# Seeding a second mask per column tile in the attention stage: ScalarE for the even key tiles, VectorE for some odd ones

## What is computed

```python
def proj(W):
    return (x @ W.T).reshape(B, S, H, D).transpose(0, 2, 1, 3)
q, k, v = (proj(Wq), proj(Wk), proj(Wv))
scores = jnp.einsum('bhsd,bhtd->bhst', q, k) * scale
scores = jnp.where(mask[None, None, :, :], -jnp.inf, scores)
attn = jax.nn.softmax(scores, axis=-1)
out = jnp.einsum('bhst,bhtd->bhsd', attn, v)
```

## Time and profile before

| | |
|---|---|
| median of three runs | 1149.29 us (1147.65 to 1151.28) |
| the profiled execution | 1151.16 us |
| its span | 1149.4 us |
| mean granted TensorE clock | 0.993 of full speed |
| PE busy | 1112.2 us |
| ACT busy | 789.9 us |
| DVE busy | 759.8 us |
| POOL busy | 509.5 us |
| mask matmuls L1191 on PE | 386 weight loads; 332 matmul records, mean 383 ns |
| mask copies L1378 on ACT | 124, mean 602 ns |
| row reductions L1646 on DVE | 512, mean 684 ns |
| exponentials L1372 on ACT | 512, mean 598 ns |

### The profile page before, as it was taken

The page is one execution under the profiler, slowest core; times in us unless marked ns, Lnnn a source line. Parts: engine busy times, 40 slices in busy tenths (PEclk is TensorE's granted clock), DMA queues, the critical chain, the costliest instruction groups (busy, mean ns, idle before and its releaser), DMA issues.

```text
span 1149.4 us, 23356 instructions
## 1 busy us (share of the span) xinstructions
PE 1112.2 (97%) x7466; PEld 780.0 (68%) x7520; DVE 759.8 (66%) x2265; ACT 789.9 (69%) x1752; POOL 509.5 (44%) x837
## 2 busy tenths in 40 slices
PE   8899999999999999999899999989999999999988
PEld 4333434445344453444339999979999999999968
DVE  5887786787867878678744443455555555677547
ACT  2478787887878878788596567646666666666645
POOL 7413254756747567575643663552222222232220
PEclk9999999999999999999899999999999999999999
DMA  8663938558475583754747699664566666633536
GB/s 216 191 198 124 278 122 243 163 175 257 136 229 179 170 241 131 233 179 141 262 135 232 196 278 335 194 149 117 156 181 201 194 194 204 206 54 64 166 92 220
DMA packets 101617, 213.66 MB, mean 186 GB/s; under 512 B 10917, under 2 KB 71341, under 8 KB 93046
## 3 DMA queue, kind: packets, MB, share of 16 engines
q1 hardware_dynamic: 86038, 192.42, 52.6%
q0 software_dynamic: 14304, 18.69, 8.8%
q10 hardware_dynamic: 1152, 1.05, 0.4%
HBM read 239.28 MB, written 74.29 MB: 273 GB/s over the span
## 4 chain that ended last, share of the span: by engine, by line
PE 62%; DMA 5%; issue 4%; POOL 4%; DVE 3%; ACT 2%; another core or an unknown queue 0%; POOLq 0%; DVEq 0%; ACTq 0%
PE bank L1104 31%; PE bank L1206 6%; PE bank L1173 6%; PE bank L1187 5%; DMA x<-yout,rows 4%; PE bank L1191 3%; PE bank L1150 2%; PE bank L1159 1%; PE bank L1224 1%; PE bank L1119 1%; PE bank L1264 1%; POOL x L1993 1%; ACT pt L1372 1%; PE bank L1244 1%; DVE junk L1646 1%
## 5 line engine op out<-in xcount | busy, mean ns | idle before, releaser
L1646 DVE CUSTOM_DVE_ANT_0 junk<-bank,mneg 128x512 bf16<-128x512 f32 x512 | 332.3, 684 | 110.6 <-PE bank L1173 107.9
L1372 ACT ACTIVATE pt<-bank 128x512 f32<-128x512 f32 x512 | 294.2, 598 | 64.1 <-PE bank L1187 25.9
L1993 POOL DMA_INDIRECT x<-yout,rows x78 | 123.8, 1587 | 298.6 <-ACT yout L1456 252.1
L1104 PE MATMUL bank<-hid,w 128*128 128x256 f32 x1872 | 243.7, 287 | 4.7 <-DVE hid L1794 4.7
L1104 PEld LDWEIGHTS bank<-hid,w 128*128 128x128 f32 x1872 | 230.4, 191 | 6.7 <-issue 4.8
L1794 DVE TENSOR_TENSOR hid<-full,hid 128x256 fp32r<-128x256 f32 x312 | 134.2, 436 | 140.3 <-ACT full L1451 134.7
L1446 ACT ACTIVATE hid<-bank,biases 128x256 fp32r<-128x256 f32 x312 | 150.5, 482 | 96.1 <-PE bank L1104 88.7
L1451 ACT ACTIVATE full<-bank,biases 128x256 f32<-128x256 f32 x312 | 149.8, 480 | 0.5 <-DVE hid L1794 0.5
L1191 PE MATMUL bank<-mneg,identb 128*128 128x512 bf16 x332 | 127.2, 383 | 0.0
L1206 PE MATMUL bank<-pt,vaug 128*17 128x512 f32 x1024 | 123.3, 599 | 1.8
L1104 PE MATMUL bank<-w,hid 128*128 128x256 f32 x936 | 122.3, 284 | 2.7 <-DVE hid L1794 2.7
(11 more groups left out here) (184 smaller groups left out, 1459.9 us busy)
## 6 DMA issues: line engine op xcount, KB each, us to landing
w<-split_weights SPq DMA_DIRECT2D x80, 1024.0 KB
w<-split_weights SPq DMA_DIRECT2D x40, 2048.0 KB
split_weights<-w_parts SPq DMA_DIRECT2D x64, 512.0 KB
w_parts<-in_W SPq DMA_DIRECT2D x64, 256.0 KB
split_parts<-parts SPq DMA_DIRECT2D x28, 384.0 KB, 2.6
rows<-routed SPq DMA_DIRECT2D x39, 258.0 KB, 4.1
stacks<-split_parts SPq DMA_DIRECT2D x36, 256.0 KB, 6.8
qst<-split_parts SPq DMA_DIRECT2D x24, 256.0 KB, 6.3
```

The lines of the kernel that those rows point to most:

```text
L1104: product = T.matmul(ps, w[p], x[q], start=(k == 0 and n == 0), stop=(k == len(weights) - 1 and n == 2))
L1372: A.activation(pt[n % len(pt)][:, :], ps[:, :], ACT.Exp, scale=float(D) ** -0.5).then_inc(exped.sem, 1)
L1646: V.tensor_tensor_reduce(junk[n % 2][:, :], ring_bank(step)[0][:, :], mneg[:, 0, st, :], 1.0, FLOOR, ALU.add, ALU.max, rowmax[gi % 2][:, h ...
L1993: G.indirect_dma_start(x2_dram, bass.IndirectOffsetOnAxis(ap=rows[j % NS][:, tt, E + 1:E + 2].bitcast(U32), axis=0), yout[j % NY][:, tt], ...
```

## The change

More column products are seeded, and fewer L1191 are issued.

- In key tiles 0 and 2 of groups 1 to 31, ACT seeds two products in place of one: head 3 as before, and head 1. The added copy stands behind the exponential of head 3 of the tile before.
- In key tiles 1 and 3 ACT seeds head 0 as before. In those groups whose number modulo 4 is 0 or 1, below group 30, DVE seeds one more, head 2: a `tensor_copy` of the mask (128 x 512, bf16 to f32 in PSUM) behind the reduction of the row product two before the one that precedes it (`ROWS_AHEAD` = 3). It waits for the masks and for the bank's earlier user, and counts up a semaphore of its own, `seeded_too`, on which the product then waits.
- For DVE a product counts as seedable only if the bank's earlier user lies at least three row (or column) products back (`early`).

Counted through the order of the steps, ACT has 186 copies in place of 124 (62 more, two for each of 31 groups), DVE has 30 new ones (two for each of the groups 1, 4, 5, 8, 9, ... 28, 29), and L1191 is issued 386 - 92 = 294 times.

```diff
+ROWS_AHEAD = 3
...
-    seed_after = {}
+    rows_before, n = {}, 0
+    for step in order:
+        n += step[0] == "row"
+        if step[0] == "col":
+            rows_before[step[1:]] = n
+
+    def early(user, at):
+        if user[0] == "row":
+            return row_place[user[1:]] <= rows_before[at] - ROWS_AHEAD
+        return user[0] == "col" and col_place[user[1:]] <= col_place[at] - ROWS_AHEAD
+
+    seed_after, seed_behind = {}, {}
     for gi in range(1, GROUPS):
         for kt in range(ST):
-            for hh in ((3, 2, 1, 0), (0, 1, 2, 3))[kt % 2]:
-                place = col_place[gi, kt, hh]
+            by_vector = kt % 2 and gi % NG < 2 and gi < GROUPS - 2
+            many = kt % 2 == 0
+            free = []
+            for hh in ((3, 1, 2, 0), (0, 2, 1, 3))[kt % 2]:
                 user = ring_before(("col", gi, kt, hh))
-                if user[0] == "row" or user[0] == "col" and col_place[user[1:]] <= place - SEED_AHEAD:
-                    seed_after[cols_at[place - SEED_AHEAD]] = gi, kt, hh
-                    break
+                if user[0] == "row" or user[0] == "col" and col_place[user[1:]] <= col_place[gi, kt, hh] - SEED_AHEAD:
+                    free.append((gi, kt, hh))
+            for at in free[:2 if many else 1]:
+                seed_after[cols_at[col_place[at] - SEED_AHEAD]] = at
+            for at in [at for at in free[1:] if by_vector and early(ring_before(("col", *at)), at)][:1]:
+                seed_behind[rows_at[rows_before[at] - ROWS_AHEAD]] = at
...
-                seed = (gi, kt, hh) in seeded.value
-                if seed:
+                seed = (gi, kt, hh) in seeded.value or (gi, kt, hh) in seeded_too.value
+                if (gi, kt, hh) in seeded.value:
                     pe.wait_ge(*seeded.at((gi, kt, hh)))
+                elif seed:
+                    pe.wait_ge(*seeded_too.at((gi, kt, hh)))
                 else:
                     pe.wait_ge(*freed)
...
                                        rowmax[gi % 2][:, hh, st:st + 1]).then_inc(max_found.sem, 1)
+                after = seed_behind.get((gi, hh, st))
+                if after:
+                    ps, freed = ring_bank(("col", *after))
+                    dve.wait_ge(masks_made, MASKS)
+                    dve.wait_ge(*freed)
+                    V.tensor_copy(ps[:, :], mneg[:, 1, after[1], :]).then_inc(seeded_too.sem, 1)
```

More of the change, by code:

```diff
@@ L765, in ring_before @@
         return ring_users[n] if n >= 0 else None
-    seed_after = {}
+    rows_before, n = {}, 0
[8 more added lines that the diff above has]
+    seed_after, seed_behind = {}, {}
     for gi in range(1, GROUPS):
         for kt in range(ST):
-            for hh in ((3, 2, 1, 0), (0, 1, 2, 3))[kt % 2]:
-                place = col_place[gi, kt, hh]
+            by_vector = kt % 2 and gi % NG < 2 and gi < GROUPS - 2
+            many = kt % 2 == 0
+            free = []
+            for hh in ((3, 1, 2, 0), (0, 2, 1, 3))[kt % 2]:
                 user = ring_before(("col", gi, kt, hh))
-                if user[0] == "row" or user[0] == "col" and col_place[user[1:]] <= place - SEED_AHEAD:
-                    seed_after[cols_at[place - SEED_AHEAD]] = gi, kt, hh
-                    break
+                if user[0] == "row" or user[0] == "col" and col_place[user[1:]] <= col_place[gi, kt, hh] - SEED_AHEAD:
[4 more added lines that the diff above has]
+                seed_behind[rows_at[rows_before[at] - ROWS_AHEAD]] = at
     seeded = signal("seeded", [seed_after[at] for at in cols_at if at in seed_after])
+    seeded_too = signal("seeded_too", [seed_behind[at] for at in rows_at if at in seed_behind])
     project_place = {at: n for n, at in enumerate(projects)}
```

## The result

Over 20 runs each, the changed kernel took 1151.68 us (1149.17 to 1155.24) and the kernel before 1148.37 us (1145.09 to 1153.49): ratio 1.0029, 95% interval 1.0018 to 1.0041. The forecast was 1140.6 us, 0.8% faster. Leaving out 92 mask matmuls bought nothing: the kernel is 2 to 5 us slower.

The account below looks back on a forecast made before the run. PE's own issue was taken to set the pace from about 75 to 510 us; 15.4 - 2.3 - 0.9 - 1.5 - 2.0 = 8.7 us gained, taking the median from 1149.29 to 1140.6 us, range 1133 to 1148.

Parts of the forecast that it names:

- what bounds the kernel: Steady part, about 75 to 510 us: PE's own issue sets the pace, busy 68.44 us of 69.
- displaced eviction: Steady groups: evictions queued on ACT behind the new copy move back by up to 0.5 us, mostly absorbed by idle time.
- The ceiling: All of attention: 92 mask matmuls removed at 0.22 us each, 20.2 us, reached only where PE sets the pace.
- the ring bank: Groups 3 to 25: a bank freed late makes PE stand, 0.1 us per group, 2.3 us lost (bounds 0 and 6.9).
- DVE's copies: Steady part: 0.61 us each in DVE's queue, 0.1 to 0.3 us to spare, no further loss charged.
- Rival (c): DVE copy too long for its place, 1.38 us, at 24 steady places and the last part: slower, 1155.4 us; chance 0.06.
- The start: Groups 1 and 2: products waiting for copies lose 2.2 us against 1.3 won, -0.9 us net.
- 510 to 599 us: Last part of attention: 1.5 us charged from 510 to 575 us and 2.0 us from 575 to 599 us.
- The stretch at half clock: Within 510 to 575 us, PE at 1.2 GHz: a longer or missing stretch would move the time some 4 us.
- the 0.50 us for each copy at the end: 575 to 599 us: four new copies in ACT's full queue at 0.50 us each, 2.0 us lost.
- (b): Steady tiles: ScalarE becomes the bound, each group giving up 0.4 us in place of 0.1; 1147.5 us; chance 0.14.

## Why the prediction was wrong

- **The step that failed first, what bounds the kernel: wrong for half of each batch.** "PE's own issue sets the pace from about 75 to 510 us" was read from PE alone. The places of 0.1 and 0.3 us where PE did wait were passed over as small. By the table above POOL's chain already set the length of a batch, with DVE waiting 0.12 us for it; without the chain PE needed 72.06 us. That matmuls hardly wait shows that PE is nearly the last at every place, not that another engine has slack. The averages hid it: POOL is busy for 43.57 us of 69, but without a gap for 23 of them. The prediction had no sentence on POOL in the steady part. This and the displaced eviction below make up the whole miss there: 5.8 us gained against 13.1 forecast, and 7.5 more once POOL's work is short.
- **The ceiling: right in size, wrong in where it applies.** 0.22 us a mask holds: outside the chain 6 masks give 1.26 us (70.95 against 72.21), or 1.31 by the rests. The section cited from the Trainium skill, 131 ns a matmul, would give 0.79; the runs speak for the row. Of 12 masks in a steady batch six lie inside the chain and give nothing.
- **The other step that failed: the displaced eviction.** The prediction named the ranks' eviction as queued behind the new copy, reckoned that the DVE copy ahead pushes the reduction back to 351.8, and charged the ring bank, 0.1 us for each group, since ACT's idle time "takes most of it up". The lateness (1.11 us) was nearly seen; its consumer was missed. What counts is not the ring bank but POOL, whose chain starts there. This costs 0.9 us in a batch (71.83 against 70.95), 1.1 by the rests.
- **DVE's copies: price right, loss half right.** 0.69 us, the nearest row; PE's weight loads waited 1.0 us in all for them from 75 to 510 us. By themselves they lost nothing in the steady part, but ahead of ACT's copy they made 0.59 of the 1.11 us by which the ranks were late. Rival (c), a copy of over 1.2 us, didn't occur.
- **The start: right in kind**, +1.3 in place of +0.9 us.
- **510 to 599 us: right in kind, too small.** 3.5 us charged; the copies cost 4.7, the total is +6.0. The mis-sized term is the 0.50 us for each copy at the end: it was the occupancy of ACT's queue, and the products started 0.9 to 1.3 us late. The stretch at half clock is there in both profiled executions, with a mean of 0.73 from 556 to 575 us, and explains no difference between them.
- **The rivals.** The measured 1151.68 us lies between (b), 1147.5, and (c), 1155.4, and nearer to (c), whose mechanism didn't occur. Rival (b) came closest in mechanism, a queue on ACT, but had it wrong: not ACT's occupancy, but one instruction's place in its queue, and POOL. No rival named POOL.

The terms measured in the table add up to +1.5 us, the profiled spans differ by -0.7, and the runs by +3.3 (2 to 5). The step from +1.5 to -0.7 comes from stretches that the change doesn't touch: the changed kernel was 0.6 us quicker up to group 1 and 1.6 us quicker behind the last column product. In the 13 profiled executions on record this last stretch took 546.7 to 552.2 us, so a difference of 1 or 2 us between two single executions means little. For the +3.3 the 20 executions of the changed kernel say something. Ten have a mean granted clock of 0.990 or more, as the profiled one has (0.993), and a median of 1150.6 us, 2.2 above the kernel before; the other ten have 0.987 or 0.988 and a median of 1153.7. Among the 43 executions of the kernel before that were timed beside the experiments, one is below 0.990. So part of the 3.3 us goes with a lower clock in half of the executions; why the changed kernel has it more often is not shown.

## What to carry to other kernels

Before crediting a saving on the busiest engine, ask of every other engine how long it works without a gap and what waits for its end. A wait of 0.1 us once in a period is a warning: here it meant that half of a batch could not get shorter. For each instruction that an insertion pushes back, follow its consumer, not the engine's idle time: 0.93 us of work cost 1.0 us ahead of one eviction and nothing behind it. To test such a chain, measure its length and the batch's in every period: if the difference is constant, the chain sets the pace. And a copy that is ready early in one stretch can be late in another of the same loop, so seed only where the product doesn't wait.

## What the runs showed of the hardware

Two prices that were bounds before: a DVE copy of 128 x 512 from bf16 to f32 in PSUM takes 0.69 us, as long as the reduction with two operands, although it reads one; and the next DVE instruction starts 0.60 us after it (all 30 copies of the changed kernel). And the same chain of 42 instructions on POOL took between 22.71 and 23.59 us; a wait of 0.82 us for an indirect transfer made the longest.
